# An expert layer, attention and a second expert layer: the first expert phase routed in two halves, larger memory pieces, the middle reordered

## The reference

```python
x = x + 0.5 * ffn(layernorm(x))
x = x + attention(layernorm(x))          # 16 heads of width 8, low-rank weights, full softmax
x = x + 0.5 * ffn(layernorm(x))

def ffn(x):                              # x: (2048, 128)
    shared = (silu(x @ sg) * (x @ su)) @ sd             # inner width 256
    logits = x @ gate_w                                 # 32 experts
    e, score = argmax(logits), sigmoid(max(logits))     # one expert a token
    xs = x * score
    routed = (silu(xs @ g[e]) * (xs @ u[e])) @ d[e]     # each token with its own expert's weights
    return shared + routed
```

## Time and profile before

| | |
|---|---|
| median of 3 runs | 646.51 us (644.31 to 647.37) |
| profiled execution | 639.84 us, span 638.1 us |
| busy share of the span | PE 86%, DVE 71%, ACT 60%, POOL 23% |
| first routing, start to first turn | 0 to 63.0 us |
| first phase's turns and last stores | 63.0 to 135.1 us |
| turnover and attention | 135.1 to about 518 us |
| second routing | about 511 to 559.3 us |
| second phase's turns, tail | 559.3 to 638.1 us |

### The profile page before, as it was taken

One profiled execution on the slowest core, in us unless ns is written; L12 is line 12 of the kernel. 1 busy time (PEld: TensorE's weight loads), 2 busy tenths in 40 slices (PEclk: granted clock), 3 DMA queues, 4 the chain that ended last, 5 costly groups with the idle time before them and its releaser, 6 DMA issues.

```text
span 638.1 us, 13759 instructions
## 1 busy us (share of the span) xinstructions
PE 545.6 (86%) x4592; PEld 213.9 (34%) x4593; DVE 453.0 (71%) x832; ACT 381.3 (60%) x814; POOL 147.9 (23%) x236
## 2 busy tenths in 40 slices
PE   2983999935578999999999999999999977899991
PEld 2642344413221222222222222222224434534440
DVE  6561334436479899999999999999996567434442
ACT  2210344414322899999999999999997744134440
POOL 2563144534330000000000000000000034214552
PEclk9997899977655899999999999999999999889997
DMA  9997232221451000100001010000000001112114
GB/s 233 320 334 219 75 88 85 69 79 43 132 168 43 13 2 3 51 2 26 29 2 52 3 50 5 3 2 2 3 2 2 1 19 35 34 33 60 51 38 142
DMA packets 52655, 40.69 MB, mean 64 GB/s; under 512 B 5257, under 2 KB 49950, under 8 KB 52592
## 3 DMA queue, kind: packets, MB, share of 16 engines
q1 hardware_dynamic: 49520, 35.58, 19.2%
q0 software_dynamic: 3072, 4.28, 2.0%
HBM read 26.85 MB, written 14.88 MB: 65 GB/s over the span
## 4 chain that ended last, share of the span: by engine, by line
PE 71%; DVE 13%; DMA 6%; issue 4%; ACT 2%; POOL 2%; SPq 1%; POOLq 0%; ACTq 0%; DVEq 0%
PE bank L1399 22%; PE pair L1376 18%; PE pair L1264 8%; PE bank L1281 5%; DVE rowmax L1031 4%; PE pair L1273 3%; DMA xe<-rows 3%; PE pair L1124 2%; PE bank L1187 2%; POOL rows L514 2%; PE pair L1116 2%; ACT oT L747 1%; PE bank L1252 1%; PE bank L1388 1%; PE bank L1330 1%
## 5 line engine op out<-in xcount | busy, mean ns | idle before, releaser
L1031 DVE TENSOR_REDUCE rowmax<-pair 128x1 f32<-128x1024 f32 x256 | 294.6, 1217 | 15.6 <-PE pair L1376 15.5
L734 ACT ACTIVATE arena<-bank 128x512 f32<-128x512 f32 x500 | 271.1, 597 | 30.7 <-PE bank L1388 23.6
L1376 PE MATMUL pair<-k_stack,q_stack 48*128 48x512 bf16 x512 | 162.7, 403 | 11.0 <-DVE rowmax L1031 10.1
L1399 PE MATMUL bank<-arena 128*32 128x256 f32 x2048 | 161.3, 393 | 3.1 <-ACT oT L747 0.7
L1388 PE MATMUL bank<-q_stack,k_stack 51*128 51x512 bf16 x500 | 152.2, 387 | 0.4 <-ACT arena L734 0.4
L521 POOL DMA_INDIRECT y<-yb,slot_token x64 | 62.9, 982 | 97.9 <-ACT yb L647 94.0
L981 DVE TENSOR_TENSOR arena<-pair,arena 128x256 f32<-128x256 f32 x64 | 27.2, 425 | 78.9 <-ACT arena L642 70.6
L1399 PEld LDWEIGHTS bank<-arena 128*32 128x32 f32 x2048 | 43.4, 108 | 98.5 <-issue 63.5
L1264 PE MATMUL pair<-w_exp,xeT 128*64 x128 | 68.7, 619 | 0.4 <-ACT xeT L637 0.4
L1266 PE MATMUL pair<-w_exp,xeT 128*64 128x512 f32 x128 | 68.7, 619 | 0.0
L1376 PEld LDWEIGHTS pair<-k_stack,q_stack 48*128 48x128 bf16 x512 | 28.4, 95 | 117.8 <-DVE rowmax L1031 83.8
(11 more groups left out here) (187 smaller groups left out, 579.8 us busy)
## 6 DMA issues: line engine op xcount, KB each, us to landing
xe<-rows SPq DMA_DIRECT2D x64, 66.0 KB
w_exp<-in_r_gate SPq DMA_DIRECT2D x4, 1024.0 KB, 10.8
w_exp<-in_r_up SPq DMA_DIRECT2D x4, 1024.0 KB, 10.7
w_exp<-in_r_down SPq DMA_DIRECT2D x8, 512.0 KB, 10.6
rows<-empty_row SPq DMA_DIRECT2D x1, 2112.0 KB, 11.4
rows<-empty_row SPq DMA_DIRECT2D x32, 66.0 KB, 3.5
xnT<-y SPq DMA_DIRECT2D x8, 256.0 KB, 3.4
q_parts<-arena SPq DMA_DIRECT2D x12, 128.0 KB, 2.2
```

Source lines behind the costliest of these rows:

```text
L734: nc.scalar.activation(prob[c % 2 * GH + head_of(u, c, k)], ring_bank("score", STEPS * u + i), ACT.Exp, scale=SCALE).then_inc(prob_ready, 1)
L1031: nc.vector.tensor_reduce(rowmax[u % 2][:, m:m + 1], pair[j % 2][:, :], AX_X, ALU.max).then_inc(smax_read, 1)
L1376: ins = nc.tensor.matmul(pair[j % 2][:, part * BANK:(part + 1) * BANK], q_stack[r][rows, half, l, t * P:(t + 1) * P], k_stack[r][rows, l, ...
L1399: ins = nc.tensor.matmul(bank[6][32 * h:32 * (h + 1), cols], v_grp[u % 2][:, c, h, :], prob[c % 2 * GH + h][:, cols], start=(c == 0 and w ...
```

## The change

1. **First phase in two halves.** `TILES_OF` has four parts instead of three: tiles 0 to 7 and 8 to 15 in the first phase, the first three quads and the last in the second. The first half is normalised, scored, ranked and placed by the rule that the first three quads of the second phase followed; the second half follows as the last quad there does (`ranks_behind`, `more_pages`, with three operations more in each `place_quad`). `choose` gives its first step to a function `tops`; the four small operations become `used_pages`. `page_owners` always takes both regions, five small operations instead of three.
2. **The last quad's shared expert in the first phase** runs after the turns (`SH_AHEAD = (3, 4)`, `sh_late`), in front of attention. For that y comes back into parts of `q_stack[0]` and `q_stack[3]` instead of `xnT`. The residual add of y waits for the shared expert's add; PE's transposes of the next norm wait for its last product.
3. **Larger pieces.** A token's place changes: partition p of a half holds tokens 8p to 8p+7 of that half, so that x, y and the output move as 2048 contiguous bytes a partition and quad (512 before). The blank rows of the first phase go out four at a time (2112 bytes, 528 before). The down weights are read as pairs of rows (1024 bytes, 512 before) in 4 transfers instead of 8; `product` therefore writes its 256 columns alternately into two halves.
4. **Order.** `store_norm` of the last unit stands after the first `place_quad` of the second routing. In the second phase `sh_silu` and `sh_product` number 3 stand ahead of the last quad's choice. In the first phase SP issues the first four loads of gathered rows together and the four clears behind them. POOL's `clear_stacks` stands after the scatters instead of ahead of them.

The diff, cut to its core:

```diff
-TILES_OF = ((0, TILES), (0, FIRST_TILES), (FIRST_TILES, TILES))
+TILES_OF = ((0, TILES // 2), (TILES // 2, TILES), (0, FIRST_TILES), (FIRST_TILES, TILES))
...
+    def quad_rows(rows, g):
+        part = rows[g // 2 * BATCH_TILES * P:(g // 2 + 1) * BATCH_TILES * P, :].rearrange("(p t) h -> p t h", t=BATCH_TILES)
+        return part[:, 4 * (g % 2):4 * (g % 2) + 4, :]
...
-            sp.dma_start(rows_dram[0].rearrange("(j p) r -> p j r", p=P),
-                         empty_row[:, :].unsqueeze(1).broadcast_to([P, TURNS, ROW])).then_inc(prefilled[0], 16)
+            sp.dma_start(rows_dram[0].rearrange("(p j k) r -> p j (k r)", p=P, k=BLANKS),
+                         blank_rows.unsqueeze(1).broadcast_to([P, SLOTS // P // BLANKS, BLANKS * ROW])).then_inc(prefilled[0], 16)
...
-                for c in range(2):
-                    sp.dma_start(w3[:, e:e + step, 2 * INNER + c * P:2 * INNER + (c + 1) * P],
-                                 r_down[e:e + step, c * P:(c + 1) * P, :].rearrange("e p h -> p e h")).then_inc(experts_loaded, 16)
+                sp.dma_start(w3[:, e:e + step, 2 * INNER:],
+                             r_down[e:e + step].rearrange("e (p c) h -> p e (c h)", c=2)).then_inc(experts_loaded, 16)
...
                 for r in range(4):
                     load(r, r)
+                if n == 0:
+                    for r in range(4):
+                        clear(r)
...
-                    sp.dma_start(y_back[:, quad(g), :], y_view[:, quad(g), :]).then_inc(y_loaded[g], 16)
+                    sp.dma_start(y_back[g], quad_rows(y_dram[n], g)).then_inc(y_loaded[g], 16)
...
-            clear_stacks()
             ffn(0)
...
+                if n == 0:
+                    clear_stacks()
...
+            def sh_late(n):
+                for i in range(2 * SH_AHEAD[n], 2 * QUADS):
+                    sh_silu(n, i)
...
+            def used_pages():
+                nc.vector.tensor_scalar(full_to[:, :], count_i[:, :], float(PAGE), None, ALU.add)
+                nc.vector.tensor_copy(more_i[:, 0:1], spare_to[:, EXPERTS:EXPERTS + 1])
+                after(nc.vector.tensor_tensor(spare_2[:, :], spare_at[:, :], count_i[:, :], ALU.subtract))
+                after(nc.vector.tensor_tensor(spare_2[:, :], spare_2[:, :], base_e[:, :], ALU.subtract))
...
                 if n == 0:
-                    normalize(0)
+                    normalize(0, 0, 2)
+                    normalize(0, 2, 4)
+                    tops(0)
                     choose(0)
                     chances(0)
+                    weigh_rows(0)
+                    tops(1)
+                    spare_pages(0)
+                    place_quad(0, 0)
+                    place_quad(0, 1)
                     sh_product(0, 0)
-                    weigh_rows(0)
-                    spare_pages(0)
-                    for g in range(QUADS):
-                        place_quad(0, g)
-                        if g < 3:
-                            sh_product(0, g + 1)
+                    used_pages()
+                    choose(1)
+                    chances(1)
+                    weigh_rows(1)
+                    sh_product(0, 1)
+                    more_pages(1)
+                    place_quad(1, 2)
+                    sh_product(0, 2)
+                    place_quad(1, 3)
+                    sh_product(0, 3)
...
                     sh_product(1, 2)
-                    choose(2)
+                    sh_product(1, 3)
+                    tops(3)
+                    choose(3)
...
-                    nc.vector.tensor_tensor(h_sb[r % 2], bank[r % 2][:, INNER:2 * INNER], silu_sb[r % 2][:, 0:INNER],
-                                            ALU.mult).then_inc(h_done, 1)
+                    by_pair = lambda a: a.rearrange("p (i c) -> p i c", c=2)
+                    nc.vector.tensor_tensor(h_sb[r % 2].rearrange("p (c i) -> p i c", c=2), by_pair(bank[r % 2][:, INNER:2 * INNER]),
+                                            by_pair(silu_sb[r % 2][:, 0:INNER]), ALU.mult).then_inc(h_done, 1)
...
             def attention():
+                for i in range(2 * SH_AHEAD[0], 2 * QUADS):
+                    sh_product(0, i)
                 normalize(1, 0, 2)
+                for q in range(SH_AHEAD[0], QUADS):
+                    sh_add(0, q)
...
-                for g in range(QUADS - 1):
-                    place_quad(1, g)
-                nc.vector.tensor_scalar(full_to[:, :], count_i[:, :], float(PAGE), None, ALU.add)
...
+                place_quad(2, 0)
                 store_norm(UNITS - 1)
+                place_quad(2, 1)
+                place_quad(2, 2)
+                used_pages()
...
                     logits(0, QUADS - 1)
-                    sh_up(0)
                     ranks(0)
-                    sh_up(1)
-                    sh_up(2)
-                    sh_up(3)
-                    sh_down(0)
+                    sh_up(n, 0)
+                    ranks_behind(1)
+                    sh_up(n, 1)
+                    ranks(1)
+                    sh_up(n, 2)
+                    sh_up(n, 3)
+                    sh_down(n, 0)
+                    sh_up(n, 4)
+                    sh_up(n, 5)
                     page_owners()
-                    sh_up(4)
-                    sh_up(5)
...
+            def sh_late(n):
+                pe.wait_ge(y_done, TURNS * (n + 1))
+                for i in range(2 * SH_AHEAD[n], 2 * QUADS):
+                    sh_up(n, i)
+                for q in range(SH_AHEAD[n], QUADS):
+                    sh_down(n, q)
```

More of the change, by code:

```diff
@@ L26 @@
 ROW = P + 4
+BLANKS = 4
+BATCH_TILES = TILES // 2
 NOWHERE = 4 * TOKENS
 EPS = 1e-5
+SH_AHEAD = (3, 4)
 RSQRT_SEED = 0x5F3759DF
@@ L820, in normalize @@
                 else:
-                    for g in range(QUADS):
+                    for g in range(first, last):
                         dve.wait_ge(x_loaded[g], 16)
@@ L895, in place_quad @@
             def place_quad(k, g):
-                n, q = min(k, 1), quad(g)
+                n, q = k // 2, quad(g)
                 first, _ = TILES_OF[k]
@@ L1140, in ranks, with ranks_behind @@
                                          start=(t == 0), stop=(t == last - 1))
-                nc.tensor.matmul(own, before[:, :], here, start=(k < 2), stop=False)
-                blocks = last - first + (k == 2)
+                nc.tensor.matmul(ranks_at[k], before[:, :], here, start=not behind, stop=False)
+                blocks = last - first + behind
                 for d in range(1, blocks):
-                    ins = nc.tensor.matmul(ranks_bank[k][:, d * EXPERTS:blocks * EXPERTS], onesb[:, :], here[:, 0:(blocks - d) * EXPERTS],
+                    ins = nc.tensor.matmul(ranks_area[k][:, d * EXPERTS:blocks * EXPERTS], onesb[:, :], here[:, 0:(blocks - d) * EXPERTS],
                                            start=False, stop=(d == blocks - 1))
                 ins.then_inc(ranks_ready, 1)
-            def ranks_behind():
-                pe.wait_ge(slots_ready, 2 * QUADS - 1)
-                for t in range(FIRST_TILES):
-                    hot = onehot[1][:, t * EXPERTS:(t + 1) * EXPERTS].unsqueeze(1).broadcast_to([P, 5, EXPERTS])
-                    nc.tensor.matmul(bank[3][:, 0:5 * EXPERTS].rearrange("p (b e) -> p b e", e=EXPERTS), onesb[:, :], hot,
+            def ranks_behind(k):
+                first, last = TILES_OF[k]
+                blocks = last - first + 1
+                if k == 3:
+                    pe.wait_ge(slots_ready, 2 * QUADS - 1)
+                for t in range(first):
+                    hot = onehot[k // 2][:, t * EXPERTS:(t + 1) * EXPERTS].unsqueeze(1).broadcast_to([P, blocks, EXPERTS])
+                    nc.tensor.matmul(ranks_area[k][:, 0:blocks * EXPERTS].rearrange("p (b e) -> p b e", e=EXPERTS), onesb[:, :], hot,
                                      start=(t == 0), stop=False)
@@ new lines, in sh_up @@
+            def sh_up(n, i, parts=(0, 1)):
+                q, c = i // 2, i % 2
+                for part in parts:
+                    if part == 0:
+                        at_least(pe, shh_sb, 8 * n + i - 1)
+                    ins = nc.tensor.matmul(sh_bank(n, c, part), w_sh[:, part * INNER + c * P:part * INNER + (c + 1) * P],
+                                           xnT[:, q * BANK:(q + 1) * BANK], start=True, stop=True)
+                    if part == 1:
+                        ins.then_inc(shg_ps, 1)
@@ new lines, in sh_down @@
+            def sh_down(n, q, first=0, last=4):
+                pe.wait_ge(shh_sb, 8 * n + 2 * q + 2)
+                if q < SH_AHEAD[n]:
+                    at_least(pe, shy_added, 4 * n + q)
+                for t in range(first, last):
+                    for c in range(2):
+                        ins = nc.tensor.matmul(shy_bank(n, q)[:, t * P:(t + 1) * P], h_sh[q % 2][c][:, t * P:(t + 1) * P],
+                                               w_sh[:, 2 * INNER + c * P:2 * INNER + (c + 1) * P], start=(c == 0), stop=(c == 1))
```

(2 more changed lines are left out.)

221 lines of the change are left out of this document (107 added, 114 removed).

## The result

The changed kernel takes 636.96 us (median of 4 runs, 635.68 to 637.31) against 646.2 us of the kernel before beside it (644.31 to 647.37): a ratio of 0.9855, interval 0.9831 to 0.9878. A second series gave 0.9818 (0.9798 to 0.9839). The forecast was 635.5.

The account below looks back on a forecast made before the run. Bound: the first routing's POOL scatters, with weight loads beside them, and PE's waits in the second routing. 4.7 + 0.1 + 0 + 5.2 + 1.0 = 11.0 us off the 646.51 median gives 635.5, range 632 to 639.

Parts of the forecast that it names:

- the bounds that it lists for 629: Whole kernel: low end of the wider range, from upper bounds of parts 1, 4, 5 and half of part 3.
- Part 1: First routing: routing in halves starts POOL's scatters 5.15 us earlier; first turn at 58.3 instead of 63.04, 4.7 us gained.
- The pause of POOL: First routing: after eight scatters POOL waits once, some 0.8 us, for quad 2 to be placed at 39.0.
- part 3: First phase's turnover: the shared expert's last quad runs after the turns; taken as 0, with 1.6 us either way.
- Part 2: First-phase loads: larger pieces end the memory stream at 52.9 instead of 57.5 us; no gain of its own.
- The rival of the stream's old length: First routing: the weights stream keeps its length, first turn at 60.1, 1.8 us lost, 637.3; chance 0.10.
- part 6: Turns: VectorE's product writes alternately into two halves; taken as 0.42 us, costing nothing up to 1.27 us.
- Part 4: Second routing: earlier last norm and shared product bring the first turn to 553.5 instead of 559.25; 5.2 us, bounds 2.4 to 5.8.
- statistics, root, rows, scores and choice follow it unchanged: Second routing, last quad: work behind quad 3's projection keeps its pace, so the projection's 3.4 us gain carries through.
- the middle keeps a stall: Second routing: projection waits for slots, or PE runs slowly after pauses; 2.8 us less gain, 638.3; chance 0.10.
- Part 5: Tail: y returns and output leaves in 2048-byte pieces instead of 512; 1.0 us gained, between 0 and 1.8.
- The slower rival: Turns: alternating write stretches the product over 1.27 us in some 62 steady turns; 662 us at 1.7 us; chance 0.06.

Follow-up runs that it names:

- the second trace: The kernel before, run again unchanged for another trace: 646.24 us, 0.9987, span 645.7.
- the gap: Changed kernel; in the second phase GpSimd scatters the first quad, then waits for the last quad's transposed rows before scattering on: 629.79 us, 0.9791.
- the old order: Changed kernel with the gap behind the first quad's scatters and the middle ordered as before: 636.83 us, 0.9851.
- the second pair: Both kernels run again unchanged for another trace each: kernel before 646.24 us, changed kernel 636.36 us (0.9818).
- old middle: Changed kernel with the last unit's norm and the fourth shared product of the second routing put back as before: 636.81 us, 0.9874.
- held back: Changed kernel with all 16 scatters of the second phase waiting until the last quad has its slots: a single execution of 642.6 us.
- the second gap kernel: Changed kernel; in the second phase GpSimd scatters two quads, then waits for the last quad's transposed rows: 629.5 us, 0.9782.

## Why the prediction was right, point by point

**The base.** The sum was made against an execution of 639.84 us and carried over to the median with its 6.7 us added. That choice decided the result: the profiled time that the sum gave, 628.8, was 8.5 us too low, the median 1.5. It had no working behind it, since what the 6.7 us were was not known, so it was luck; the second trace shows them as later releases in both routings and longer second turns. One sum in the prediction is wrong: the bounds that it lists for 629 add up to 631.0 (635.5 less 2.3, 0.6, 0.8 and 0.8). The forecast does not rest on it.

**Part 1, 4.7 us.** The mechanism held: first scatter 28.20 (forecast 28.65), quad 2's slots at 37.71 (39.0), the last scatter at 48.41 (48.7), the first turn at 58.03 (58.3). The pause of POOL that was forecast did not come: one scatter took 2.00 us where the others take 0.96 and filled that time, so the last scatter is partly right by luck. Against the first trace it gained 5.0. Against the second it is 6.7, since there the shared expert set the first turn; three of the four traces of the kernel before and its variants start their turns at 64.7 to 65.7. So the late quad of part 3 is what lets the scatters count for the first turn: with it put back that is at 61.35. What is left of this at the end of the kernel the runs do not resolve.

**Part 2.** The stream ended near 52.6, as worked out, and the larger pieces of the blank rows buy no time: with small ones the first turn is at 57.93 as before. Those of the down weights and of x were not tested apart. The rival of the stream's old length, an end at 57.5, was not met; an end at 55.5 still cost nothing. The rule from the Trainium skill ("DMA: Bandwidth & Descriptors", Specifications), line rate from 512 bytes on, which was weighed there, does not fit these rows: 210 GB/s at 528 bytes, 295 with the 2112-byte pieces in the same window.

**Part 3, 0.** Last store to first `oT`: 94.22 and 94.30 in the first pair, 0.6 better in the second. The first turns themselves became 1.0 us longer in both pairs. Over all traces they last 69.9 to 71.8 us with the dense product and 70.8 to 72.8 with the strided one, so part 6 is a suspect; no run tests it apart from the time of the first turn.

**Part 4, 5.2 us: the step that failed.** The order works as forecast until the last quad's transposes, 3.7 us early. The step "statistics, root, rows, scores and choice follow it unchanged" is where it breaks: the scores wait until the row of 12 scatters is through, and that row begins with the first quad's slots in either order. I had the scatters only as work that must be done in time, not as work that stops TensorE's readers. Measured: 0.5 us lost against the first trace, 2.2 won against the second, 0.3 in the changed kernel by undoing it. With the gap the term is there: the last quad has its slots 21.4 us behind the last `oT` instead of 24.9 with the old order, 3.5 us sooner where 3.4 was forecast, and the page owners' transpose comes 6.6 us sooner (22.6 against 29.2). The first turn gains 6.0 (42.64 to 36.59), a little above the upper bound of 5.8, but a later stand in each of the two is mixed in. This was the rival "the middle keeps a stall", with another cause than the two named.

**Part 5, 1.0.** 0.4 and 0.5 measured: the last y took 4.17 us from issue to landing by the chain, no less than the 4.14 of before, in spite of pieces four times as large.

**Part 6, 0.** The product takes 0.62 us and not 0.42, which still fits into the wait that was counted on. It ends 0.65 us ahead of the transpose where the dense one ended 0.85 ahead, and steady turns are 1.93 us in both. The penalty that the Trainium skill states ("SBUF — State Buffer", SBUF: two separate sides) would explain half as much again; that it is the cause no run tests. The slower rival needed more than 1.27 us. Whether the term is really 0 is open, as said under part 3.

So the total came out within 1.5 us by luck. In the second pair the middle gave 3.0 us less than the sum had, the tail 0.5 and the first turns 1.0; the first routing gave 1.9 more, and the second turns 2.3 and the turnover 0.6 that the sum had at nothing.

## What to carry to other kernels

When the profiled execution is well off the median, take a second trace before costing anything: the stalls that an ordinary execution has may be missing from the one that you read. A wait that ends at "remote", behind an engine whose work is long done by the record, is worth lining up against what else begins and ends there; moving the suspect, here by holding the scatters back, settled what the rows alone could not. And a reorder on the critical path must be followed past its last step to the next thing that starts at a fixed event.

## What the runs showed of the hardware

The signals of TensorE's work come late while GpSimd issues a long row of indirect scatters, one every 1.27 us:

| trace | row of scatters, us | work done by the record | reader goes on |
|---|---|---|---|
| before, 1st | 520.0 to 535.0 (12) | 534.66 | 534.70 |
| before, 2nd | 521.7 to 536.7 (12) | 536.55 | 538.90 |
| changed, 1st | 516.0 to 531.0 (12) | 527.03 | 533.18 |
| changed, 2nd | 515.4 to 530.3 (12) | 526.38 | 532.63 |
| old middle | 515.2 to 530.2 (12) | 530.04 | 532.37 |
| held back | 534.1 to 554.1 (16) | 548.48 | 554.60 |
| gap | 513.4 to 518.3 (4) | 524.21 | 524.24 |
| gap, next row | 525.6 to 541.0 (12) | 536.50 | 538.46 |
| changed, 1st, first phase | 28.2 to 49.4 (16) | 45.75 | 51.64 |

The rows of four held nothing up, and behind the one row of eight, in the second gap kernel, the transposes were taken over 0.5 us late (525.17 to 525.63); in those of 12 and 16 it is mostly the work towards their end. That TensorE goes on and only its signals are late is argued from one trace (the whole shared expert ahead of the turns); its ends in the traces are modelled. Open: through what the scatters do this, and why the first trace of the kernel before, with the same rows, has no stand. A stand costs twice: TensorE has no record from 45.75 to 52.48 in the changed kernel's first trace, the granted clock is 0.50, 1.2 GHz, when it resumes (52 to 54 us in the window above), and the next down block takes 3.75 us instead of 2.05.
